# Second attention of a two-layer decoder block: the sum of a token's four gathered rows moved from VectorE into PSUM

## The chip, the cores and the metric

The kernel runs on one core of a Trainium2 chip. The metric is the time of one execution on the device in microseconds (us), the median of several runs; lower is better. TensorE (PE; its weight loads PEld) multiplies into PSUM, VectorE (DVE) and ScalarE (ACT) compute, GpSimd (POOL) computes and issues indirect DMAs (gathers), SyncE (SP) issues plain DMAs. Each engine runs its own program in order and waits on semaphores.

## The reference

For x of 128 sequences x 64 tokens x 128, in f32, and a context of the same shape:

```
x = x + attention0(layernorm(x), ctx, ctx)     # 16 heads of 8
x = x + ffn0(layernorm(x))                     # 32 experts, top 4, clipped swiglu, + own input
x = x + attention1(layernorm(x), ctx, ctx)     # 16 heads of 8, with rotary positions
x = x + ffn1(layernorm(x))                     # 8 experts, top 2
```

The first expert layer leaves its results as rows of a table in memory, one row per (token, expert) slot. A token's result is the sum of its four rows; that sum is added to x when the second attention starts.

## The kernel before

The 8192 tokens are 64 tiles of 128; X, the residual, stays in SBUF. The program is six stages, one after the other: attention 0, a sort of the slots, experts 0, attention 1, another sort, experts 1. The change lies in attention 1 alone (`attention(layer=1)`, about 868 to 1345 us of the profile).

An attention works on a pair of tiles at a time, 32 pairs, in a software pipeline that is written out by hand: each engine has a `body(i, on)` that is emitted for one value of i after the other, and in body i works on several pairs at once. `i.at(k)` is pair i+k, and `on(k)` says that this pair exists. Bodies run from -4 (on GpSimd from -5) to the end. The stages of pair n, with the body in which they run:

- Body n-5, GpSimd: the rows of pair n are gathered from the table `slot_results` into `gb`, of which there are two (even and odd pairs). There are eight indirect DMAs (L413) of 128 rows x 512 bytes, four ranks x two tiles. The order on GpSimd in body i (`body_with_gathers`) is: gather rank 0 of pair i+5, `scale_outputs` of pair i-2 (L455), gather rank 1, `scale_inputs` of pair i+3 (L426, L431), gather rank 2, `keep_top` of pair i-4, gather rank 3. Before rank 0 it waits until the buffer's former pair has been added to X.
- Body n-4, VectorE: `combine` waits for all eight gathers, sums the four rows (L549, a reduce over the rank) into `rows_sum` and adds them to X (L553).
- Body n-3, VectorE: `stats` of X (L528 to L541); GpSimd: `scale_inputs`, the power -0.5 of the variance, which waits for `stats`.
- Body n-2: ScalarE normalises, TensorE transposes X and the context (`inputs`, L912 and L914) into the bank `M_`.
- Body n-1: projections into `P_` and, with rotated weights, into `M_` (L919 and L920 in both cases); VectorE `rotate` (L618 twice in pairs, L629); ScalarE spreads keys and queries over the heads (L707).
- Body n: `scores` (L837), on VectorE four maxima (`score_unit`, L570), on TensorE their transposes (`maxima`, L848), transposed scores (`turned`, L862 and L874), ScalarE's exponentials.
- Body n+1: `values` (L893, L899), VectorE `divide` (L610, L612), TensorE `output`, VectorE `add_output` (L634) and `output_stats`.
- Body n+3: the rows for the next expert layer are transposed (`rows_turned`, L950, into the first half of `M_`), copied by ScalarE (L785, semaphore `tt`), and TensorE multiplies the gate (L962); then VectorE reads the logits (L585) and chooses the top 8.

The order on TensorE in body i (`body_with_rotation`) is: scores(i), values(i-1), projections(i+1) into `P_`, rows_turned(i-3), maxima(i), turned(i), projections(i+1) into `M_`, gate(i-3), next_values(i+1), output(i-1), inputs(i+2). The order on VectorE (`body_with_sums`) is: four score_unit(i), divide(i-1), the first half of the rotary product of pair i+1, rotate(i+1), read_logits(i-3), stats(i+3), combine(i+4), add_output(i-1), choose(i-3), output_stats(i-1).

`M_` is thus used by rows_turned, by the rotation and by inputs in turn, and its second half (columns 256 to 511) is free between inputs and the rotation.

Of the kernel before, what the change touches and what calls it, by code (L numbers as in the profile page):

```python
# [22 lines left out]
ALU = mybir.AluOpType  # L23
ACT = mybir.ActivationFunctionType
AX = mybir.AxisListType

P = 128
B, S, D = 128, 64, 128
# [10 lines left out]
E0, K0, F0 = 32, 4, 128  # L39
# [52 lines left out]
def hold(eng, sem, value):  # L92

    eng.wait_ge(sem, value)
    eng.nop(nofuse=True)  # L95


def build(nc, a, out, ts, ys, bias_parts):

    with ExitStack() as ctx:  # L100
# [9 lines left out]
        X = sb("X", [P, TILES, D])  # L110
# [12 lines left out]
        def part_of(name):  # L123
# [4 lines left out]
        ident, cos, sin, gate_w, max_to, den_of, bias_t, head_of, gate_b = (  # L128
            part_of(n) for n in ("ident", "cos", "sin", "gate_w", "max_to", "den_of", "bias_t", "head_of", "gate_b"))
# [19 lines left out]
        def carve(width, dt=F32):  # L149
            lo = place[0]  # L150
            place[0] += width if dt in (F32, I32, U32) else (width + 1) // 2
            assert place[0] <= ARENA, place[0]
            v = arena[:, lo:place[0]]
            return v if dt == F32 else v.bitcast(dt)
# [143 lines left out]
        gathered = [sem(f"gathered{q}") for q in range(2)]  # L298
# [6 lines left out]
        s = {n: sem(n) for n in names}  # L305

        def attention(layer):
# [19 lines left out]
                                               ("rs1", 2))}  # L327

            gb = carve2(2 * K0 * D) if layer else None
            rows_sum = carve(2 * D) if layer else None  # L330

            wq, wk, wv, wo = (Wm[:, 4 * layer + n, :] for n in range(4))
            bq, bk = bias_t[:, 2 * layer:2 * layer + 1], bias_t[:, 2 * layer + 1:2 * layer + 2]
# [2 lines left out]
            U_, O_, R_, M_, P_ = bank[0:4], bank[4], bank[5], bank[6], bank[7]  # L336
            base = layer * ITERS

            def tiles(buf, i):
                return buf[:, bass.ds(i.n * 2, 2), :]  # L340
# [20 lines left out]
            with nc.Block() as block:  # L361
# [43 lines left out]
                def _(pool):  # L405
                    def gather(i, k):

                        if k == 0 and i.n >= 2:

                            hold(pool, s["combined"], i.n - 1)  # L410
                        for j in range(2):
                            at, to = i.n * 2 + j, (j * K0 + k) * D
                            nc.gpsimd.indirect_dma_start(  # L413
                                out=gb[i.par][:, to:to + D], out_offset=None, in_=ys,
                                in_offset=bass.IndirectOffsetOnAxis(ap=slot[:, at, k:k + 1], axis=0),
                            ).then_inc(gathered[i.par], 16)
# [107 lines left out]
                def _(dve):  # L524
# [19 lines left out]

                    def combine(i):

                        q = i.par
                        hold(dve, gathered[q], (i.half + 1) * 16 * 2 * K0)
                        nc.vector.tensor_reduce(rows_sum.rearrange("p (i d) -> p i d", i=2),  # L549
                                                gb[q].rearrange("p (i k d) -> p i d k", i=2, k=K0), AX.X, ALU.add  # L550
                                                ).then_inc(s["row_sum"], 1)
                        hold(dve, s["row_sum"], i.n + 1)
                        nc.vector.tensor_tensor(tiles(X, i), tiles(X, i), rows_sum.rearrange("p (i d) -> p i d", i=2),  # L553
                                                ALU.add).then_inc(s["combined"], 1)

                    def offsets(i):

# [8 lines left out]
                    def score_unit(i, r):  # L566

                        g4 = i.g * UNITS
                        dve.wait_ge(s["score_psum"], g4 + r + 1)
                        nc.vector.tensor_reduce(mx[:].rearrange("p (w c) -> p w c", w=2)[:, :, 32 * r:32 * r + 4],  # L570
                                                U_[r][:, :].rearrange("p (w j k) -> p w j k", w=2, j=4), AX.X, ALU.max
                                                ).then_inc(s["score_max"], 1)
# [90 lines left out]
                    def body_with_sums(i, on):  # L663
                        nx, pv, p3 = i.at(1), i.at(-1), i.at(-3)
                        if on(0):
                            for r in range(UNITS):
                                score_unit(i, r)
                        if on(-1):
                            divide(pv)
                        if on(1):  # L670
                            dve.wait_ge(s["qk_psum"], nx.g + 1)
                            if not (isinstance(nx.n, int) and nx.n < 1):

                                dve.wait_ge(s["rope"], nx.n)
                            weigh(nx, QKe, P_, bq, bk, cos, "qk")
                            rotate(nx)
                        if on(-3):
                            read_logits(p3)
                        if on(3):
                            hold(dve, s["combined"], i.at(3).n + 1)  # L680
                            stats(i.at(3), small["st_a"], small["mv_a"], "stats_a", "moments_a")
                        if on(4):
                            combine(i.at(4))
                        if on(-1):
                            add_output(pv)
                        if on(-3):
                            choose(p3)
                        if on(-1):
                            output_stats(pv)
# [118 lines left out]
                def _(pe):  # L808
# [97 lines left out]
                    def inputs(i):  # L906

                        q = i.par
                        pe.wait_ge(ctx_in[q], (i.half + i.base // 2 + 1) * 16)
                        pe.wait_ge(s["normed"], i.g + 1)  # L910
                        for w in range(2):
                            nc.tensor.transpose(M_[:, w * P:(w + 1) * P], ctx_t[q][:, w * P:(w + 1) * P], ident[:])  # L912
                        for w in range(2):
                            last = nc.tensor.transpose(M_[:, (2 + w) * P:(3 + w) * P],  # L914
                                                       xn[q][:, w * P:(w + 1) * P], ident[:])
                        last.then_inc(s["cx_psum"], 1)

                    def projections(i, out_, wq, wk, done):
                        nc.tensor.matmul(out_[:, 0:2 * D], wq, CX[i.par][:, 2 * D:4 * D], start=True, stop=True)  # L919
                        nc.tensor.matmul(out_[:, 2 * D:4 * D], wk, CX[i.par][:, 0:2 * D], start=True, stop=True  # L920
                                         ).then_inc(done, 1)
# [24 lines left out]
                    def rows_turned(i):  # L946

                        pe.wait_ge(s["t_ready"], i.g + 1)
                        for w in range(2):
                            last = nc.tensor.transpose(M_[:, w * P:(w + 1) * P],  # L950
                                                       t[i.par][:, w * P:(w + 1) * P], ident[:])
                        last.then_inc(s["tt_psum"], 1)
# [13 lines left out]
                    def body(i, on):  # L966
# [31 lines left out]
                        if on(1):  # L998
                            next_values(nx)

                    def body_with_rotation(i, on):
                        ex, nx, pv, p3 = (i.at(k) for k in (2, 1, -1, -3))
                        if on(0):
                            scores(i)
                        if on(-1):
                            values(pv)
                        if on(1):
                            pe.wait_ge(s["cx"], nx.g + 1)
                            if on(0):

                                pe.wait_ge(s["vbd"], i.g + 1)
                            projections(nx, P_, wq, wk, s["qk_psum"])
                        if on(-3):
                            rows_turned(p3)
                        if on(-2):

                            pe.wait_ge(s["added"], pv.g)
                        if on(0):
                            maxima(i)
                            turned(i)  # L1020
                        if on(1):
                            if on(-3):

                                pe.wait_ge(s["tt"], p3.g + 1)
                            projections(nx, M_, Wm[:, 8, :], Wm[:, 9, :], s["rot_psum"])
                        if on(-3):
                            gate(p3)
                        if on(1):
                            next_values(nx)
                        if on(-1):  # L1030
                            if on(-3):

                                pe.wait_ge(s["logits"], p3.g + 1)
                            output(pv)
                        if on(2):
                            if on(1):

                                pe.wait_ge(s["rot"], nx.n + 1)
                            inputs(ex)

                    if not layer:
# [843 lines left out]
```

## Time and profile before

| | |
|---|---|
| Time, median of 3 runs | 1830.72 us (1826.79 to 1831.70) |
| Profiled execution: time / span | 1834.56 us / 1831.9 us |
| Mean granted TensorE clock | 0.92 |
| Busy over the whole span | PE 81%, PEld 60%, DVE 63%, ACT 49%, POOL 60% |
| Gathers of attention 1 (L413) | 256, 254.3 us of GpSimd |
| Row sums (L549) | 32, median 1940 ns |

Busy time is a sum over stages that have different limits, so the table says what each engine has to do and not which of them is waited for. The span counts from the first to the last instruction of the profiled execution. The granted clock is 1.00 at 2.4 GHz and 0.50 at 1.2 GHz. A row of busy time gives a stretch and its length, then the busy time of PE, PEld, DVE, ACT and POOL (with instructions), the granted clock, the DMA share and GB/s. A timeline row gives start, duration, engine, line, what is written from what, how many instructions were merged into it, and in brackets the idle time of that engine before it with what ended it.

### The profile page before, as it was taken

What the parts mean: (1) busy time and instruction counts of PE and PEld (TensorE: products, weight loads), DVE (VectorE), ACT (ScalarE), POOL (GpSimd) and SP (SyncE); (2) the same over time, 40 slices, a digit from 0 to 9 for tenths busy, and PEclk for the clock granted to TensorE, in tenths of its full rate; (3) what the DMA queues carried; (4) which work ended last, traced back from release to release, by engine and by line L of the source; (5) the groups of instructions that cost most, each with busy time, mean ns of one, the idle gap of its engine ahead of it and who ended that gap; (6) DMA issues with size and microseconds to landing.
All of it is one profiled execution on the core that took longest, in us unless ns stands there. A gap on an engine that the chain in (4) does not pass through costs nothing. (4 is left out here: it accounts for less than half of the span.)

```text
span 1831.9 us, 58162 instructions
## 1 busy us (share of the span) xinstructions
PE 1479.6 (81%) x21070; PEld 1104.2 (60%) x21071; DVE 1158.7 (63%) x3147; ACT 889.3 (49%) x2010; POOL 1102.3 (60%) x1438
## 2 busy tenths in 40 slices
PE   5999999739699999997277777777864799999960
PEld 4677777514477777775155555555642677777740
DVE  5777777679566666664378888888869222224432
ACT  2666666546233333332156666666545344444420
POOL 4677777400577777772777777677310776445766
PEclk9999999869899999998599999999985899999985
DMA  4211111000144444446242222112100233233332
GB/s 168 72 42 40 37 43 35 20 8 1 47 102 111 106 107 107 106 100 73 55 155 56 56 60 56 53 54 59 29 16 1 65 86 81 59 59 85 105 94 75
DMA packets 146836, 122.98 MB, mean 67 GB/s; under 512 B 27403, under 2 KB 132011, under 8 KB 145963
## 3 DMA queue, kind: packets, MB, share of 16 engines
q0 software_dynamic: 26112, 55.30, 13.8%
q1 hardware_dynamic: 120382, 65.58, 11.9%
q8 instruction: 68, 1.11, 0.3%
q10 hardware_dynamic: 240, 0.70, 0.1%
q14 instruction: 34, 0.28, 0.1%
HBM read 80.28 MB, written 41.23 MB: 66 GB/s over the span
## 5 line engine op out<-in xcount | busy, mean ns | idle before, releaser
L1427 POOL DMA_INDIRECT arena<-expert_rows,token_of_slot x432 | 415.7, 962 | 325.4 <-issue 219.8
L413 POOL DMA_INDIRECT arena<-slot_results,slot x256 | 254.3, 994 | 115.0 <-issue 86.5
L1800 DVE TENSOR_TENSOR arena<-bank,arena 128x352 f32<-128x352 f32 x144 | 74.7, 523 | 214.1 <-ACT arena L1779 213.9
L1733 PE MATMUL bank<-W,arena 128*128 x576 | 196.4, 464 | 0.9 <-ACT arena L1791 0.9
L1525 PE MATMUL bank<-W,arena 128*128 x576 | 175.4, 400 | 0.0
L699 ACT ACTIVATE arena<-bank 128x512 f32<-128x512 f32 x256 | 132.2, 603 | 87.4 <-PE bank L874 87.4
L570 DVE TENSOR_REDUCE mx<-bank 128x8 f32<-128x512 f32 x256 | 158.2, 679 | 13.7 <-PE bank L837 10.1
L1383 POOL DMA_INDIRECT arena<-slot_results,slot x128 | 121.5, 949 | 59.3 <-issue 43.3
L436 POOL TENSOR_TENSOR arena<-arena,fixed 128x1024 f32<-128x1024 f32 x64 | 121.4, 1917 | 55.8 <-ACT arena L717 55.8
L1747 PEld LDWEIGHTS bank<-W,arena 128*128 128x128 f32 (+1 forms) x864 | 114.2, 190 | 37.7 <-issue 30.2
L1747 PE MATMUL bank<-W,arena 128*128 (+1 forms) x864 | 120.5, 275 | 1.8 <-ACT arena L1786 1.8
L1733 PEld LDWEIGHTS bank<-W,arena 128*128 128x128 f32 x576 | 99.2, 192 | 32.8 <-issue 2.8
L707 ACT ACTIVATE arena<-arena,fixed 128x256 f32<-128x256 f32 x256 | 105.7, 495 | 26.3 <-DVE arena L629 26.3
L1353 PE MATMUL bank<-arena 128*128 128x288 f16 (+1 forms) x384 | 86.1, 394 | 39.1 <-ACT arena L1338 21.4
L1610 DVE TENSOR_SCALAR arena<-bank 128x256 f32<-128x256 f32 x144 | 61.1, 424 | 86.1 <-PE bank L1525 85.2
L1560 PE MATMUL bank<-W,arena 128*128 x576 | 114.2, 319 | 0.0
L610 DVE RECIPROCAL arena<-bank 128x256 f32<-128x256 f32 x64 | 111.7, 1746 | 2.4 <-PE bank L899 2.4
L1779 ACT ACTIVATE arena<-bank 128x352 f32<-128x352 f32 x144 | 66.7, 463 | 92.7 <-PE bank L1733 92.7
L1525 PEld LDWEIGHTS bank<-W,arena 128*128 128x128 f32 x576 | 89.6, 196 | 21.9 <-issue 1.7
L1785 ACT ACTIVATE arena<-bank 128x256 f32<-128x256 f32 x144 | 55.2, 383 | 84.6 <-PE bank L1758 84.6
L1560 PEld LDWEIGHTS bank<-W,arena 128*128 128x128 f32 x576 | 86.7, 190 | 10.4
L837 PE MATMUL bank<-arena 32*64 32x256 f32 x2048 | 72.6, 388 | 24.6 <-ACT arena L707 24.2
(197 smaller groups left out, 3468.7 us busy)
## 6 DMA issues: line engine op xcount, KB each, us to landing
slot_results<-arena SPq DMA_DIRECT2D x108, 256.0 KB
arena<-in_ctx SPq DMA_DIRECT2D x64, 128.0 KB
expert_rows<-arena SPq DMA_DIRECT2D x64, 128.0 KB, 1.9
arena<-expert_rows,token_of_slot POOLq DMA_INDIRECT x432, 2.6
arena<-slot_results,slot POOLq DMA_INDIRECT x384, 2.5
X<-in_x SPq DMA_DIRECT2D x32, 128.0 KB, 2.2
W<-in_w SPq DMA_DIRECT2D x4, 1024.0 KB
out_x<-arena SPq DMA_DIRECT2D x32, 128.0 KB, 1.8
```

The lines of the kernel that those rows point to most:

```text
L413: nc.gpsimd.indirect_dma_start(out=gb[i.par][:, to:to + D], out_offset=None, in_=ys, in_offset=bass.IndirectOffsetOnAxis(ap=slot[:, at, k: ...
L436: nc.gpsimd.tensor_tensor(dst[i.par].rearrange("p (b j k) -> p b j k", b=4, j=4), src[i.par].rearrange("p (b k) -> p b k", b=4).unsqueeze( ...
L570: nc.vector.tensor_reduce(mx[:].rearrange("p (w c) -> p w c", w=2)[:, :, 32 * r:32 * r + 4], U_[r][:, :].rearrange("p (w j k) -> p w j k", ...
L610: nc.vector.reciprocal(rec, O_[:, 2 * D:4 * D]).then_inc(s["o_recip"], 1)
L699: nc.scalar.activation(Pt[r], U_[r][:, :], ACT.Exp, scale=SCALE).then_inc(s["probs"], 1)
L707: last = nc.scalar.activation(dst[i.par].rearrange("p (b j k) -> p b j k", b=4, j=4)[:, :, j, :], src[i.par].rearrange("p (b k) -> p b k", ...
L1383: nc.gpsimd.indirect_dma_start(out=gb[q][:, at:at + D], out_offset=None, in_=ys, in_offset=bass.IndirectOffsetOnAxis(ap=slot[:, 2 * n + j, ...
L1427: nc.gpsimd.indirect_dma_start(out=XE[n % R][:, c * ROW:(c + 1) * ROW], out_offset=None, in_=ts, in_offset=bass.IndirectOffsetOnAxis(ap=to ...
L1525: last = nc.tensor.matmul(h, XT[i.par][:, c * P:(c + 1) * P], W0a[:, bass.ds(x_e, 1), :], start=False, stop=True, skip_group_check=True)
L1560: last = nc.tensor.matmul(y, AT[pv.par][:, c * P:(c + 1) * P], W0b[:, bass.ds(x_e, 1), :], start=False, stop=True, skip_group_check=True)
L1733: last = nc.tensor.matmul(H_[2 * r + u][:, 0:F1], XT[i.par][:, c * P:(c + 1) * P], W1a[:, bass.ds(x_e, 1), u * F1:(u + 1) * F1], start=Tru ...
L1747: last = nc.tensor.matmul(Y_[j.par][:, d * P:(d + 1) * P], AT[d % 2][0:f, k * P:(k + 1) * P], W1b[0:f, bass.ds(x_e, 1), k * P:(k + 1) * P] ...
```

## The change

The four rows are summed by four matmuls with the identity, which accumulate in the second half of `M_`. They stand in TensorE's body between rows_turned and maxima (`sum_rows`), so TensorE, and no longer VectorE, waits for the gathers of pair i+4. The add of the sum to X now reads PSUM, and `combine` stands on VectorE behind the four score_unit, ahead of divide. Two waits on `combined` are new on TensorE: before the projections into `M_`, and before `inputs` where there is no such projection. `sum_rows` waits for `tt` (or, in the first bodies, for the add of the pair before). GpSimd waits for `row_sum` where it waited for `combined`.

```diff
-            rows_sum = carve(2 * D) if layer else None
...
-                            hold(pool, s["combined"], i.n - 1)
+                            hold(pool, s["row_sum"], i.n - 1)
...
                     def combine(i):
 
-                        q = i.par
-                        hold(dve, gathered[q], (i.half + 1) * 16 * 2 * K0)
-                        nc.vector.tensor_reduce(rows_sum.rearrange("p (i d) -> p i d", i=2),
-                                                gb[q].rearrange("p (i k d) -> p i d k", i=2, k=K0), AX.X, ALU.add
-                                                ).then_inc(s["row_sum"], 1)
                         hold(dve, s["row_sum"], i.n + 1)
-                        nc.vector.tensor_tensor(tiles(X, i), tiles(X, i), rows_sum.rearrange("p (i d) -> p i d", i=2),
-                                                ALU.add).then_inc(s["combined"], 1)
+                        nc.vector.tensor_tensor(tiles(X, i), M_[:, 2 * D:4 * D].rearrange("p (i d) -> p i d", i=2),
+                                                tiles(X, i), ALU.add).then_inc(s["combined"], 1)
...
                             for r in range(UNITS):
                                 score_unit(i, r)
+                        if on(4):
+                            combine(i.at(4))
                         if on(-1):
                             divide(pv)
...
-                        if on(4):
-                            combine(i.at(4))
                         if on(-1):
                             add_output(pv)
...
+                    def sum_rows(i):
+
+                        hold(pe, gathered[i.par], (i.half + 1) * 16 * 2 * K0)
+                        rows = gb[i.par].rearrange("p (i k d) -> p i k d", i=2, k=K0)
+                        for k in range(K0):
+                            last = nc.tensor.matmul(M_[:, 2 * D:4 * D].rearrange("p (i d) -> p i d", i=2), ident,
+                                                    rows[:, :, k, :], start=(k == 0), stop=(k == K0 - 1),
+                                                    skip_group_check=True)
+                        last.then_inc(s["row_sum"], 1)
...
                             rows_turned(p3)
+                        if on(4):
+                            if on(-3):
+
+                                pe.wait_ge(s["tt"], p3.g + 1)
+                            elif far.n > 0:
+
+                                pe.wait_ge(s["combined"], far.n)
+                            sum_rows(far)
...
+                            if on(4):
+
+                                pe.wait_ge(s["combined"], far.n + 1)
                             projections(nx, M_, Wm[:, 8, :], Wm[:, 9, :], s["rot_psum"])
...
                                 pe.wait_ge(s["rot"], nx.n + 1)
+                            elif on(4):
+
+                                pe.wait_ge(s["combined"], far.n + 1)
                             inputs(ex)
```

## Rows read from the trace of the kernel before

**Rows 1.** Busy time by stretch: the pipeline filling, and the steady part of attention 1.

```profile
868.00:923.00 55.00, 17.88 (x169) 11.71 (x170) 17.62 (x37) 10.72 (x24) 41.99 (x47) 0.50 0.22 58
940.00:1313.00 373.00, 288.63 (x6586) 217.06 (x6586) 314.25 (x864) 235.06 (x556) 262.67 (x360) 0.97 0.23 67
```

**Rows 2.** Waits from 940 to 1240 us: total, times, longest.

```profile
PE bank L848 <- DVE mx L570: 42.8, 21, 2.2
```

**Rows 3.** Timeline of one round, 1084 to 1103 us.

```profile
1084.40 0.44 PE L848 MATMUL bank<-fixed,mx 128*128 128x128 f32 x2 [2.18 <-DVE mx L570]
...
1086.90 0.70 PE L919 MATMUL bank<-arena,Wm 128*128 128x256 f32 x2
...
1087.44 0.59 PE L920 MATMUL bank<-arena,Wm 128*128 128x256 f32 x2
...
1087.87 0.51 PE L962 MATMUL bank<-fixed,arena 128*128 128x8 f32 x4
...
1088.08 0.88 DVE L618 SCALAR_TENSOR_TENSOR arena<-bank,fixed 128x256 f32<-128x256 f32 x2 [0.82 <-PE bank L920]
...
1090.85 1.97 DVE L549 TENSOR_REDUCE arena<-arena 128x256 f32<-128x1024 f32 x1
...
1090.94 0.72 POOL L426 TENSOR_TENSOR arena<-arena,power 128x2 f32<-128x2 f32 x1 [0.44 <-DVE arena L541]
...
1091.56 1.12 PE L837 MATMUL bank<-arena 32*64 32x256 f32 x32 [0.58 <-ACT arena L707]
...
1093.03 0.43 DVE L553 TENSOR_TENSOR X<-X,arena 128x256 f32 x1 [0.21 <-DVE arena L549]
...
1093.37 0.42 DVE L634 TENSOR_TENSOR X<-bank,X 128x256 f32 x1
...
1095.43 2.47 DVE L570 TENSOR_REDUCE mx<-bank 128x8 f32<-128x512 f32 x4
...
1095.48 0.38 PE L950 MATMUL bank<-fixed,arena 128*128 128x128 f32 x2
...
1095.89 0.38 ACT L785 ACTIVATE arena<-bank 128x256 f32<-128x256 f32 x1 [0.84 <-PE bank L950]
...
1096.53 0.94 POOL L413 DMA_INDIRECT arena<-slot_results,slot  x1 [0.30 <-issue]
...
1097.96 0.44 PE L848 MATMUL bank<-fixed,mx 128*128 128x128 f32 x2 [2.10 <-DVE mx L570]
...
1101.88 0.88 DVE L618 SCALAR_TENSOR_TENSOR arena<-bank,fixed 128x256 f32<-128x256 f32 x2 [1.07 <-PE bank L920]
```

**Rows 4.** TensorE's timeline: scores that open bodies 2, 29 and 30.

```profile
940.22 1.12 PE L837 MATMUL bank<-arena 32*64 32x256 f32 x32 [1.46 <-ACT arena L707]
...
1320.39 1.12 PE L837 MATMUL bank<-arena 32*64 32x256 f32 x32 [0.58 <-ACT arena L707]
...
1332.34 1.12 PE L837 MATMUL bank<-arena 32*64 32x256 f32 x32 [0.58 <-ACT arena L707]
```

**Rows 5.** Timeline of the filling, 909 to 925 us.

```profile
909.65 0.94 POOL L413 DMA_INDIRECT arena<-slot_results,slot  x1 [0.30 <-issue]
...
912.23 1.89 DVE L549 TENSOR_REDUCE arena<-arena 128x256 f32<-128x1024 f32 x1 [5.41 <-DMA arena<-slot_results,slot]
...
917.10 0.69 PE L848 MATMUL bank<-fixed,mx 128*128 128x128 f32 x2 [3.95 <-DVE mx L570]
...
923.56 0.88 DVE L618 SCALAR_TENSOR_TENSOR arena<-bank,fixed 128x256 f32<-128x256 f32 x2 [5.74 <-PE bank L920]
```

**Rows 6.** Busy time of two neighbouring rounds; the clock is third from the end.

```profile
1176.00:1191.10 15.10, 11.82 (x252) 8.87 (x252) 12.14 (x34) 9.11 (x23) 10.03 (x15) 0.89 0.20 52
1191.10:1204.70 13.60, 10.46 (x249) 7.89 (x250) 11.64 (x34) 8.66 (x22) 10.32 (x14) 1.00 0.21 58
```

**Rows 7.** Timeline around pair 6's landing, 944 to 953 us.

```profile
944.90 0.94 POOL L413 DMA_INDIRECT arena<-slot_results,slot  x1 [0.30 <-issue]
...
952.62 1.99 DVE L549 TENSOR_REDUCE arena<-arena 128x256 f32<-128x1024 f32 x1 [0.42 <-DMA arena<-slot_results,slot]
```

More of the change, by code:

```diff
@@ L999, in body @@
                             next_values(nx)
+                    def sum_rows(i):
[6 more added lines that the diff above has]
+                        last.then_inc(s["row_sum"], 1)
                     def body_with_rotation(i, on):
-                        ex, nx, pv, p3 = (i.at(k) for k in (2, 1, -1, -3))
+                        ex, nx, pv, p3, far = (i.at(k) for k in (2, 1, -1, -3, 4))
                         if on(0):
```

## The prediction

> **What bounds the kernel now.** I read four views, in this order. First the busy time by stretch [rows 1]: the second attention's steady part (940 to 1313 us) keeps VectorE busy 314 of 373 us, TensorE 289, GpSimd 263, at a mean granted clock of 0.97; the filling of its pipeline (868 to 923) has GpSimd busy 42 of 55 us and TensorE at half clock. No engine is full, so waits decide. Second the waits [rows 2]: TensorE's longest is for the score maxima, 42.8 us in 21 rounds, some 2.0 us each. Third the timeline of one round [rows 3], which shows the loop that this wait belongs to. Call M the start of the maxima's transposes (L848), R the start of the rotation's second pair on VectorE (L618, which waited for L920). M to R is TensorE's work, 1084.40 to 1088.08 = 3.68 us (3.92 a round later, 1097.96 to 1101.88). R to the next M is VectorE's, 9.88 us, nearly without a gap: rope, statistics, the row sum (L549, 1.97), its add, the output's add, top-8, statistics, four score maxima (L570), and then L848 sets off. The scores themselves (L837) had ended at 1092.68, 2.75 us before L570 started. Last the rounds' starts by L837 [rows 4]: (1320.39 - 940.22)/27 = 14.08 us on average; a round of the tail, which has no row sum, lasts 11.95.
>
> So on this view the row sum is on the path, and taking it off should pay. The question is what the new place of the sum asks for.
>
> **The change, part by part.**
> 1. VectorE loses L549 (1.97 us) and the 0.21 us before its add, and the add (0.43) leaves the stretch R to M [rows 3]: some 2.5 us off that stretch. It would pay if nothing else ended later there.
> 2. VectorE gains an add that reads PSUM, now ahead of `divide`. L634 has the same form and lasts 0.42, 0.34 to the next start. It waits for the row sum, which ends some 0.2 us after M, where L570 ended just before M. The later chain moves by about 0.6 us, and L618 stood idle 0.82 to 1.07 for TensorE [rows 3]: free while that lasts, up to 0.6 us a round if not.
> 3. TensorE gains four f32 matmuls of 256 columns, two records each. By L919, L920 and what follows, starts lie 0.54, then 0.43 apart [rows 3]: 0.54 + 3 x 0.43 = 1.83 us. Bounds: 1.72 and 2.16. Ahead of them it waits for `tt` (L785, to 1096.27), which costs 0.4 to 0.65 after L950's stream. That alone fits into the wait of 2.10 us before L848, nearly.
> 4. The waits on `combined` before the second rotation matmuls and before `inputs` cost nothing in the steady part: the add ends some 0.7 us after M, L919 starts 2.50 after it. The write to X[pair] beside them is as before.
> 5. GpSimd waits for `row_sum` in place of `combined` before it fills a buffer again: both came a round earlier, no cost.
> 6. What decides: `sum_rows` in body i needs all eight gathers of pair i+4, and it is now held on TensorE ahead of the maxima, before the middle of the body, where `combine` had them at its end. GpSimd issues the last four of these gathers in its body i-1, behind `scale_inputs` of pair i+2 (L426), and L426 waits for VectorE's statistics of that pair, which come after R of body i-1. In [rows 3]: R at 1088.08, L426 at 1090.94 released by L541, the last gather (L413) at 1096.53 to 1097.47. From the start of a last gather to the row sum that waited for it, 909.65 to 912.23 = 2.58 us, 1.64 after its end [rows 5]. So pair i+4 lands at R + 2.86 + 6.53 + 1.64 = R + 11.03. TensorE gets there once L785 has ended, 1096.27, that is R + 8.2: it waits 2.8 us more, and behind it in TensorE's order stand the maxima's transposes, `turned` and the rotation, for which R itself waits. It is a loop through four engines and a DMA, and GpSimd can't run ahead, since L426 needs this round's R. Before, the reduce sat some 5.8 us behind the landing (about 1104.9, one mean round after L549's 1090.85, against 1099.1), so this loop had slack.
>
> **The sum.** A round in the new loop: M to R 3.68, to L426 2.86, to the end of the last gather 6.53, landing 1.64, start of the matmuls 0.06, the sum 1.83: 16.60 us. With M to R at the mean of both rounds shown (3.80) 16.7. I add 0.4 for the clock (below): 17.1, against 14.08 before, +3.0.
> The clock: TensorE stood idle 2.1 us before the maxima, and rounds with a stretch at 0.5 exist already; the one shown has a mean clock of 0.89 and 15.1 us, where its neighbour at 1.00 has 13.6 [rows 6], so a low stretch costs about 1.3 us (1.1 to 1.5). The new idle time, from the end of L950 (1095.86) to the landing, is 3.3 us. More low stretches must follow; I take one in three rounds beyond what there was, 0.4 us, between 0 and 1.3. By the Trainium skill (TensorE: Matmul & The Clock Gate, HAM oscillation), TensorE falls back to half speed when the gap between two bursts grows long enough, and does so in every round of such a loop; by that rule the sum would take the 1.3 and not the 0.4. The rows of before agree that gaps bring low stretches, but not in every round.
> Filling: pairs 0 to 3 are taken as they land, at GpSimd's pace, both before and after. But in body -1 the rotation now waits for pair 3: landed 912.23 [rows 5], four sums at half clock 3.6, the add 0.5, two rotation matmuls about 2: R(-1) at 918.3. Pair 4 lands 11.0 later, 929.3; sums at half clock, M(0) at 933; before it was 917.10. M(0) to R(0) was 6.46 at half clock; 5.5 if the clock rises earlier. R(0) is at 938.5 against 923.56: +15 (11 to 17).
> Weights: while the second layer's expert weights are loaded (4.5 MB by their shapes), pair 6, whose last gather started at 944.90, was taken at 952.62, 7.7 us later in place of 2.58 [rows 7]. Before, this had slack; now one round takes it: +5 (0 to 6).
> Tail: bodies 28 on have no sum on either side; body 28's maxima lose their old wait: -2.
> Total: 27 x 3.0 = 81.5, +15 +5 -2 = +99.5 us. The profiled execution's span is 1831.9, its time 1834.6, and the three runs' median, 1830.7, is 3.8 below that. So 1931 in span, and 1930 us by the median.
>
> By the Trainium skill (DMA: Bandwidth & Descriptors, Anatomy of one DMA) a GpSimd-issued DMA costs about 2.0 us and its bytes over 436 GB/s; for 64 KB that is 2.15, and an estimate with that in place of the 1.64 behind the gather's end adds 0.5 a round, some 14 us in all. The row measures 2.58 from the start of the issue and 1.64 from its end, and I go by it.
>
> **Rivals.**
> - The clock falls in every round: 16.7 + 1.3 = 18.0 us a round. 27 x 3.9 = 106, +17 +5 -2 = +126: 1957 us. For it: the longer gap. Against: with a period that walks against whatever paces the clock, some rounds should escape, as 2.1 us of idle did before.
> - No more low stretches than before, cheap filling: 16.6 a round, 27 x 2.5 = 68, +11 +0 -2 = +77: 1908 us.
> - The gathers aren't late, for instance because GpSimd gets further ahead than I read: TensorE binds. Its own loop is 11.95 [rows 4] + 1.83 + 0.65 for `tt` = 14.4, +0.35 a round, 9 us and the filling's 15: 1855 us. Against: the order on GpSimd is written out, and L426 is released by L541 in the rows.
> - The other side, faster: the sum hides wholly in the wait for the maxima and VectorE's 2.5 us come off. The floor is then 11.95 + 1.83 = 13.8, -0.3 a round: with no loss in filling 1822 us. It needs the landing at or before L950's end, R + 7.8, so 3.2 us earlier than the rows have it; from there on each 1 us of lateness costs 27 us.
>
> **How the numbers follow.** Chances: forecast 0.69, clock in every round 0.15, cheap clock and filling 0.11, gathers in time 0.03, faster 0.02. The predicted time is the first's, 1930; its own range is 1915 to 1947. The range 1903 to 1960 takes in the second and third, with the bounds of M to R and of the matmuls (1.72 to 2.16, -3 to +9 us); it leaves out some 0.1. The smallest difference that counts is 0.3%, 5.5 us. Slower 0.97; faster 0.02; within 0.3% 0.01.
>
> **What the new profile would show.** Right: `sum_rows` is a TensorE group of some 256 records whose idle time before it is ended by the DMA of the gathers, 2.5 to 3.5 us in nearly each of 28 rounds; the wait of L848 on L570 is gone; the distance from a last gather's start to the first sum's start is about 2.6 us; L426 still starts some 2.9 us after L618's second pair; rounds of 16.5 to 18 us; more low stretches than in 0.97; VectorE idle most before the new add. Wrong: rounds near 14, the sum's wait ended by L785 or absent, gathers that end well before L950. If the rounds are 16.6 exactly, my clock term is at fault; if the filling costs other than 15, my chain of body -1 is.

## The result and the profile after

The changed kernel takes 1956.7 us (median of 4, 1952.5 to 1966.3) against 1830.4 before: ratio 1.068, interval 1.065 to 1.072. The profiled execution's time is 1957.4 us and its span 1955.6, 123.7 more than before.

From the page of the profile, the engines' busy time and shares of the span, and TensorE's granted clock in 40 slices:

```profile
PE 1566.7 (80%) x21326; PEld 1173.0 (60%) x21327; DVE 1099.8 (56%) x3115; ACT 889.7 (45%) x2010; POOL 1091.1 (56%) x1438
...
PEclk9999999788999999985888888889896599999985
```

Busy time by stretch (columns as in [rows 1]): the filling, the steady part, and two single rounds.

```profile
868.00:923.00 55.00, 23.22 (x96) 15.59 (x96) 6.79 (x28) 5.47 (x13) 33.72 (x40) 0.55 0.17 44
960.00:1420.00 460.00, 348.26 (x6425) 265.65 (x6424) 250.88 (x794) 221.89 (x525) 248.57 (x348) 0.88 0.18 51
1163.30:1182.50 19.20, 14.77 (x257) 11.22 (x257) 10.23 (x35) 9.09 (x22) 10.08 (x15) 0.82 0.15 41
1218.40:1234.80 16.40, 12.26 (x262) 9.58 (x263) 9.92 (x32) 8.80 (x22) 9.88 (x14) 1.00 0.17 48
```

VectorE does less, 251 of 460 us where it was 314 of 373 [rows 1], and waits. The granted clock of the steady part is 0.88, not 0.97. One of the two rounds has a clock of 0.82 and lasts 19.2 us, the other 1.00 and 16.4.

Waits from 960 to 1400 us (total, times, longest), where [rows 2] had TensorE wait for the maxima:

```profile
DVE X L547 <- PE bank L1000: 174.9, 24, 12.0
...
POOL arena L425 <- DVE arena L540: 128.1, 24, 9.3
...
PE bank L1000 <- DMA arena<-slot_results,slot: 72.7, 23, 3.3
```

The wait of the maxima's transposes on the score maxima has gone from the list. TensorE now waits for the gathers, 3.2 us in each of 23 rounds, VectorE for the sum, and GpSimd for VectorE's statistics, 5.3 us a round, which it did for 0.4 in [rows 3].

The timeline of one round, to be read beside [rows 3]. M is again the start of the maxima's transposes (now L842) and R the start of the rotation's second pair on VectorE (now L612).

```profile
1162.73 0.72 POOL L425 TENSOR_TENSOR arena<-arena,power 128x2 f32<-128x2 f32 x1 [5.38 <-DVE arena L540]
...
1163.35 1.12 PE L831 MATMUL bank<-arena 32*64 32x256 f32 x32 [0.57 <-ACT arena L701]
...
1164.71 2.48 DVE L564 TENSOR_REDUCE mx<-bank 128x8 f32<-128x512 f32 x4
...
1167.68 0.38 ACT L779 ACTIVATE arena<-bank 128x256 f32<-128x256 f32 x1 [0.84 <-PE bank L944]
...
1168.32 0.94 POOL L412 DMA_INDIRECT arena<-slot_results,slot  x1 [0.30 <-issue]
...
1170.90 3.75 PE L1000 MATMUL bank<-arena,fixed 128*128 128x256 f32 x8 [3.25 <-DMA arena<-slot_results,slot]
...
1174.44 0.63 PE L842 MATMUL bank<-fixed,mx 128*128 128x128 f32 x2
...
1174.87 0.42 DVE L547 TENSOR_TENSOR X<-bank,X 128x256 f32 x1 [7.68 <-PE bank L1000]
...
1178.87 0.88 DVE L612 SCALAR_TENSOR_TENSOR arena<-bank,fixed 128x256 f32<-128x256 f32 x2 [0.67 <-PE bank L914]
...
1181.73 0.72 POOL L425 TENSOR_TENSOR arena<-arena,power 128x2 f32<-128x2 f32 x1 [6.13 <-DVE arena L540]
```

It reads as a chain that closes on itself. GpSimd sets off (L425) at 1162.73, and 6.53 us later, at 1169.26, its last gather (L412) ends. The sum (L1000) starts at 1170.90, 1.64 after that, released by the DMA, though `tt` was there since 1168.06 (L779). From the sum's start to M are 3.54 us, at the clock's lower level (1.80 at the higher one, see below), and from M to R 4.43. L425 starts again 2.86 after R. The five stretches add up to 19.00 us, from one L425 (1162.73) to the next (1181.73). The four score maxima (L564), for which M waited before, were done at 1167.19, 7.2 us ahead of M.

The scores that open bodies 3 and 28 of the changed kernel:

```profile
978.99 1.12 PE L831 MATMUL bank<-arena 32*64 32x256 f32 x32 [1.15 <-ACT arena L701]
...
1433.18 1.12 PE L831 MATMUL bank<-arena 32*64 32x256 f32 x32 [0.57 <-ACT arena L701]
```

That is (1433.18 - 978.99)/25 = 18.17 us a round; before, by the same bodies, 14.16 (952.96 to 1306.97). The span's 123.7 us are 26.0 up to body 3, 25 x 4.0 = 100.2 from there to body 28, and -2.5 after it.

### The profile page after: what moved, and what is told of

The parts are those of the page before. It is cut to its first block and busy times, and to the rows that moved or that the text cites. A ratio compares the mean times of both kernels' runs of the same rounds, so it can differ in the third digit from the quotient of the medians.

```text
span 1955.6 us, 58655 instructions
## 1 busy us (share of the span) xinstructions
PE 1566.7 (80%) x21326; PEld 1173.0 (60%) x21327; DVE 1099.8 (56%) x3115; ACT 889.7 (45%) x2010; POOL 1091.1 (56%) x1438
## 3 DMA queue, kind: packets, MB, share of 16 engines
q0 software_dynamic: 26112, 55.30, 12.9%
## 5 line engine op out<-in xcount | busy, mean ns | idle before, releaser
L412 POOL DMA_INDIRECT arena<-slot_results,slot x256 | 246.6, 963 | 114.9 <-issue 87.5
L1000 PE MATMUL bank<-arena,fixed 128*128 128x256 f32 x256 | 107.4, 593 | 128.9 <-DMA arena<-slot_results,slot 110.7
L564 DVE TENSOR_REDUCE mx<-bank 128x8 f32<-128x512 f32 x256 | 158.5, 682 | 17.8 <-PE bank L831 17.7
L1000 PEld LDWEIGHTS bank<-arena,fixed 128*128 128x128 f32 x256 | 73.5, 300 | 152.5 <-issue 137.4
L547 DVE TENSOR_TENSOR X<-bank,X 128x256 f32 (+1 forms) x32 | 13.6, 425 | 254.6 <-PE bank L1000 254.6
L1401 POOL DMA_INDIRECT arena<-slot_results,slot x128 | 121.4, 948 | 59.6 <-issue 43.3
L425 POOL TENSOR_TENSOR arena<-arena,power 128x2 f32<-128x2 f32 x64 | 46.0, 718 | 177.6 <-DVE arena L540 175.0
L1751 PEld LDWEIGHTS bank<-W,arena 128*128 128x128 f32 x576 | 99.3, 192 | 32.9 <-issue 2.8
```

Of the source, the lines that this page charges most:

```text
L412: nc.gpsimd.indirect_dma_start(out=gb[i.par][:, to:to + D], out_offset=None, in_=ys, in_offset=bass.IndirectOffsetOnAxis(ap=slot[:, at, k: ...
L1000: last = nc.tensor.matmul(M_[:, 2 * D:4 * D].rearrange("p (i d) -> p i d", i=2), ident, rows[:, :, k, :], start=(k == 0), stop=(k == K0 - ...
L1401: nc.gpsimd.indirect_dma_start(out=gb[q][:, at:at + D], out_offset=None, in_=ys, in_offset=bass.IndirectOffsetOnAxis(ap=slot[:, 2 * n + j, ...
L1751: last = nc.tensor.matmul(H_[2 * r + u][:, 0:F1], XT[i.par][:, c * P:(c + 1) * P], W1a[:, bass.ds(x_e, 1), u * F1:(u + 1) * F1], start=Tru ...
```

## The experiments

Each was timed beside the kernel before on the same chip, whose median moved between 1834 and 1837 us, so ratios are given. In the table, "round" is the mean from body 3 to body 28 by TensorE's scores in the profiled execution, and "clock" is the granted clock of the steady part.

| kernel | time, us | ratio to before (interval) | round | body 3 starts | clock |
|---|---|---|---|---|---|
| before | 1830.4 | | 14.16 | 953.0 | 0.97 |
| changed | 1956.7 | 1.068 (1.065 to 1.072) | 18.17 | 979.0 | 0.88 |
| 1 gathers first | 1835.1 | 1.000 (0.998 to 1.002) | 14.02 | 961.2 | 1.00 |
| 2 gathers first, in before | 1825.9 | 0.995 (0.993 to 0.997) | 13.71 | 955.3 | 0.99 |
| 3 one rank | 1905.0 | 1.038 (1.035 to 1.042) | 16.26 | 973.6 | 0.91 |
| 4 wait filled | 1921.5 | 1.048 (1.045 to 1.051) | 16.54 | 982.0 | 0.99 |
| 5 place alone | 1912.9 | 1.044 (1.038 to 1.049) | 16.54 | 972.8 | 0.82 |
| 6 late sum | 1878.7 | 1.025 (1.019 to 1.030) | 14.97 | 980.1 | 0.99 |
| 7 pair adds | 1808.8 | 0.987 (0.982 to 0.993) | 13.23 | 950.3 | 0.99 |
| 8 pair adds, gathers first | 1809.4 | 0.987 (0.981 to 0.992) | 13.20 | 956.1 | 0.98 |
| 9 half in PSUM | 1812.1 | 0.988 (0.985 to 0.990) | 13.26 | 963.6 | 0.99 |
| 10 pair adds moved | 1824.5 | 0.994 (0.992 to 0.996) | 13.49 | 961.5 | 0.97 |

**1. Gathers first.** Theory: the late landing closes a loop over four engines. Rival: the sum's work and waits on TensorE.

```diff
                             gather(i.at(5), 1)
+                            gather(i.at(5), 2)
+                            gather(i.at(5), 3)
                         if on(3):
                             scale_inputs(i.at(3))
-                        if on(5):
-                            gather(i.at(5), 2)
                         if on(-4):
                             keep_top(i.at(-4))
-                        if on(5):
-                            gather(i.at(5), 3)
```

> The changed kernel with one edit on GpSimd: all four ranks of a pair's gathers are issued ahead of scale_inputs in the body, so that none of them stands behind L425's wait for VectorE's statistics. If the lateness of the gathers in the loop GpSimd - TensorE - VectorE is the cause (my theory), the wait before the sum matmuls, 3.0 to 3.3 us a round after the change, is gone, TensorE binds with 11.95 + 1.83 + 0.65 = 14.4 us a round, the low clock goes with the wait, and the time is 1845 to 1870 us. If it is what the sum adds to TensorE and its new waits on tt and combined that costs (rival), the rounds stay above 17 us and the time above 1930.

Its steady part and one round:

```profile
960.00:1300.00 340.00, 297.30 (x6268) 232.34 (x6272) 242.72 (x780) 216.91 (x513) 238.64 (x338) 1.00 0.21 58
```

```profile
1161.73 0.38 PE L942 MATMUL bank<-fixed,arena 128*128 128x128 f32 x2
...
1162.15 0.38 ACT L777 ACTIVATE arena<-bank 128x256 f32<-128x256 f32 x1 [0.96 <-PE bank L942]
...
1162.68 1.97 PE L998 MATMUL bank<-arena,fixed 128*128 128x256 f32 x8 [0.56 <-ACT arena L777]
...
1164.48 0.38 PE L840 MATMUL bank<-fixed,mx 128*128 128x128 f32 x2
...
1164.87 0.42 DVE L545 TENSOR_TENSOR X<-bank,X 128x256 f32 x1 [3.33 <-PE bank L998]
```

The sum (L998) now starts on the copy L777 with 0.56 us idle, never on a DMA, and M (L840) follows 1.80 later. The whole 6.8% is gone with the order of GpSimd's instructions; TensorE still does all four matmuls. The rival falls. The time is 10 us under the expectation's lower end, since TensorE's own loop is 14.0 and not 14.4 and the filling costs 8 us and not 15.

**2. The same reorder in the kernel before**, as a control.

> The kernel before with the same reorder on GpSimd, as a control of the reorder by itself. The reduce sat 5.8 us behind the landing, so on my theory nothing moves: 1825 to 1836 us. If the order on GpSimd is worth something of its own (rival: scale_inputs or scale_outputs come late behind eight gathers, or the filling gets longer), the time moves by more than 5 us.

The time lies in the range I gave, but the kernel before, timed beside it, took 1837.0: the reorder isn't neutral, it is worth 0.5%. The round is 13.6 us most of the time, where 13.65 and 14.0 alternated, and of the 25 rounds two have a stretch at the lower clock (15.3 and 14.9 us) where the kernel before has seven (14.9 to 15.3 us); these five rounds are over half of the gain. Set against this control, experiment 1 is 0.5% slower: what the move costs when the gathers are early.

**3. One rank.** Leaves out ranks 1 to 3 of the sum; the gathers stay.

```diff
-                        for k in range(K0):
+                        for k in range(1):
...
-                                                    rows[:, :, k, :], start=(k == 0), stop=(k == K0 - 1),
+                                                    rows[:, :, k, :], start=True, stop=True,
```

> The changed kernel with one matmul per pair in place of four; it leaves out ranks 1 to 3 of the sum. All eight gathers are still issued and waited for. If the loop through the gathers sets the round, the three matmuls lie behind the landing and on the loop: 1.3 us a round less at full clock, up to 2.6 at half, so 35 to 70 us less than the changed kernel, 1887 to 1922 us. If the matmuls were hidden and only the wait cost, the time stays at 1957.

Some 52 us less than the changed kernel: the matmuls behind the landing are on the loop. The round is 1.9 us shorter for three matmuls fewer, between their price at full (1.3) and at half clock (2.6).

**4. The wait filled** with five matmuls whose result is overwritten.

```diff
+                            if on(-3) and on(1):
+                                for _ in range(5):
+                                    nc.tensor.matmul(M_[:, 2 * D:4 * D], ident, CX[nx.par][:, 0:2 * D],
+                                                     start=True, stop=True, skip_group_check=True)
                             sum_rows(far)
```

> The changed kernel with five further matmuls of 256 columns on TensorE, between the wait on tt and the wait for the gathers, into the half of the bank that the sum then overwrites: 2.2 us of work inside a wait of 3.2. If the idle time is what brings TensorE's clock down, and this makes rounds of 18.3 out of 16.5, the added work makes the kernel faster: rounds of 16.5 to 17.3, 1905 to 1935 us, clock of the steady part above 0.94. If the low clock isn't what lengthens the round, the time stays within 5 us of 1957 or grows.

```profile
960.00:1385.00 425.00, 370.27 (x6784) 285.41 (x6769) 252.43 (x802) 225.67 (x533) 252.24 (x353) 0.99 0.20 58
```

```profile
1151.86 2.43 PE L1028 MATMUL bank<-arena,fixed 128*128 128x256 f32 x10 [0.47 <-ACT arena L779]
...
1154.74 1.97 PE L1000 MATMUL bank<-arena,fixed 128*128 128x256 f32 x8 [0.46 <-DMA arena<-slot_results,slot]
...
1156.55 0.38 PE L842 MATMUL bank<-fixed,mx 128*128 128x128 f32 x2
```

TensorE is given 2.4 us more to do each round (L1028). It waits 0.46 for the gathers in place of 3.25, the sum takes 1.81 to M (L842) in place of 3.54, and the kernel is some 35 us faster than the changed one. The round is 16.54 at a clock of 0.99, and TensorE still waits for the gathers: this is the loop without the clock. The other 1.63 us a round of the changed kernel are the clock's, which falls with the idle wait and stays up when the wait is filled.

A wait of this length doesn't bring the clock down every time. In the changed kernel 22 of the 25 rounds have a granted clock of 0.82 to 0.91, and three have 1.00, one of them this, behind a wait of 3.10:

```profile
1217.64 0.72 POOL L425 TENSOR_TENSOR arena<-arena,power 128x2 f32<-128x2 f32 x1 [5.03 <-DVE arena L540]
...
1225.85 1.97 PE L1000 MATMUL bank<-arena,fixed 128*128 128x256 f32 x8 [3.10 <-DMA arena<-slot_results,slot]
...
1227.65 0.38 PE L842 MATMUL bank<-fixed,mx 128*128 128x128 f32 x2
...
1234.14 0.72 POOL L425 TENSOR_TENSOR arena<-arena,power 128x2 f32<-128x2 f32 x1 [3.61 <-DVE arena L540]
```

From L425 to L425 it lasts 16.50 us, where the round at 0.82 lasted 19.00.

**5. The place alone.** VectorE keeps its reduce, now into two buffers in turn; `combine` moves behind the score maxima.

```diff
                                 score_unit(i, r)
+                        if on(4):
+                            combine(i.at(4))
...
-                        if on(4):
-                            combine(i.at(4))
                         if on(-1):
                             add_output(pv)
```

> The kernel before, the sum still VectorE's reduce, with combine moved to the changed kernel's place, behind the four score maxima and ahead of divide (two buffers for the row sum). TensorE gets no work. By the loop theory the place alone closes the loop: the gathers land at R + 11.0, the reduce, the add, divide and the first rotary product follow, 5.6 us, so a round lasts about 16.7 us plus what the clock loses, and the time is 1900 to 1960 us. If it is TensorE's work or its waits that make the change slow (rival), the rounds stay near 14 and the time within 15 us of 1830.

```profile
1160.73 0.94 POOL L413 DMA_INDIRECT arena<-slot_results,slot  x1 [0.30 <-issue]
...
1161.23 0.38 PE L848 MATMUL bank<-fixed,mx 128*128 128x128 f32 x2
...
1163.35 1.95 DVE L549 TENSOR_REDUCE arena<-arena 128x256 f32<-128x1024 f32 x1 [2.59 <-DMA arena<-slot_results,slot]
...
1165.53 0.42 DVE L553 TENSOR_TENSOR X<-X,arena 128x256 f32 x1 [0.23 <-DVE arena L549]
...
1168.00 1.65 DVE L618 SCALAR_TENSOR_TENSOR arena<-bank,fixed 128x256 f32<-128x256 f32 x4
...
1171.63 0.72 POOL L426 TENSOR_TENSOR arena<-arena,power 128x2 f32<-128x2 f32 x1 [3.54 <-DVE arena L541]
```

The last gather starts at 1160.73, the reduce (L549) at 1163.35, 2.62 later, released by the DMA; M (L848) isn't held and goes at 1161.23, but R, inside L618's pairs, comes behind reduce, add and divide. No work was added to TensorE, and the kernel is 4.4% slower: the ring comes from the place in the body, not from the engine. TensorE's work isn't on this ring (L618's four records run without a wait), so here its low clock, 0.82, costs nothing that shows. The round is 16.54 us where I expected 16.7 and more, the same as in experiment 4. The other 2.4% of the change's 6.8 are about what the clock costs there, 1.63 us a round.

**6. Late sum.** `sum_rows` behind turned, `combine` behind the first rotary product, GpSimd as in the changed kernel.

```diff
-                            sum_rows(far)
...
                             turned(i)
...
+                            sum_rows(far)
```

> The changed kernel with sum_rows behind turned, ahead of the rotation's projections, and combine on VectorE behind the first rotary product; the order of the gathers is as in the changed kernel. By the loop theory TensorE then comes to the sum at about R + 10.5, the gathers land at R + 11.0, and the rotation follows 3.5 us later: rounds of 14.5 to 14.9, 1840 to 1870 us, with an idle time before the sum of under 1 us. If the sum's work were the cause and not when it asks for the gathers, the time stays above 1930.

```profile
1134.75 0.38 PE L843 MATMUL bank<-fixed,mx 128*128 128x128 f32 x2
...
1135.58 0.94 POOL L412 DMA_INDIRECT arena<-slot_results,slot  x1 [0.30 <-issue]
...
1138.22 1.97 PE L1001 MATMUL bank<-arena,fixed 128*128 128x256 f32 x8 [0.58 <-issue]
...
1140.41 0.42 DVE L547 TENSOR_TENSOR X<-bank,X 128x256 f32 x1 [3.04 <-PE bank L1001]
...
1142.06 0.88 DVE L612 SCALAR_TENSOR_TENSOR arena<-bank,fixed 128x256 f32<-128x256 f32 x2 [1.22 <-PE bank L915]
```

The last gather starts at 1135.58 and the sum (L1001) at 1138.22, 2.64 later, after 0.58 us of idle. The view doesn't put this idle time to the DMA, but the distance is that of a landing (2.58 in [rows 5]), so the sum just meets it. M (L843) is free of it. The round, 14.97, is 0.1 over what I expected; the time misses by 9 us, because the filling is as long as the changed kernel's (body 3 at 980.1), which I had not put in. The sum stands some 2.9 us of TensorE's work later in the same body (from M to the end of `turned`), and that takes away 3.2 of the 4.0 us a round.

**7 and 8. Pair adds**, in the kernel before: the reduce as two plain adds. Experiment 8 has the gathers first as well.

```diff
-                        nc.vector.tensor_reduce(rows_sum.rearrange("p (i d) -> p i d", i=2),
-                                                gb[q].rearrange("p (i k d) -> p i d k", i=2, k=K0), AX.X, ALU.add
...
+                        rows = gb[q].rearrange("p (i k d) -> p i (k d)", i=2, k=K0)
+                        nc.vector.tensor_tensor(half_sum.rearrange("p (i d) -> p i d", i=2), rows[:, :, 0:2 * D],
+                                                rows[:, :, 2 * D:4 * D], ALU.add).then_inc(s["row_sum"], 1)
...
+                        nc.vector.tensor_tensor(rows_sum.rearrange("p (i d) -> p i d", i=2), halves[:, :, 0:D],
+                                                halves[:, :, D:2 * D], ALU.add).then_inc(s["row_sum"], 1)
```

> The kernel before with the reduce on VectorE (1.94 us, which reads the four ranks at a stride) split in two plain adds of 512 and 256 elements per row: 0.69 by the rope's add and 0.42, so about 0.8 us less per round where VectorE is on the path from R to M. If that path sets the round in the kernel before, as my reading had it, rounds of 13.2 to 13.4 and 1800 to 1815 us. If something else sets it (rival: the clock or GpSimd, whose round needs about 12.9), the time stays above 1820.

> The same with the gathers ahead of scale_inputs on GpSimd. The reorder alone was worth 0.5% in the kernel before, so 1792 to 1810 us if the two add up; if GpSimd's own work (8 x 1.25 us of gathers and 2.9 of powers and copies, 12.9 us) now binds, no better than the pair adds alone.

```profile
1108.74 0.69 DVE L551 TENSOR_TENSOR arena<-arena 128x512 f32<-128x512 f32 x1
1109.54 0.42 DVE L555 TENSOR_TENSOR arena<-arena 128x256 f32<-128x256 f32 x1
1110.17 0.43 DVE L558 TENSOR_TENSOR X<-X,arena 128x256 f32 x1 [0.20 <-DVE arena L555]
```

In experiment 7 the sum lasts 1.22 us (1108.74 to 1109.96) in place of 1.97, 0.75 less, and the round falls by 0.93. That is more than was taken off, because two rounds have a stretch at the lower clock where the kernel before has seven; the rounds at full clock fall from 13.8 to 13.1 on average, 0.7. So VectorE's stretch from R to M did bound the kernel before, and the change went for the right work. In experiment 8 the reorder adds nothing on top. Most of its rounds last 12.9 to 13.0 us, which is GpSimd's own pace (busy 247 of 340 us, and 0.3 us behind each issue), and two of 15.2 and 17.0 with a low clock take back what that gains.

**9. Half in PSUM.** Experiment 1, with the first half of the sum on VectorE and two matmuls.

```diff
-                        hold(pe, gathered[i.par], (i.half + 1) * 16 * 2 * K0)
-                        rows = gb[i.par].rearrange("p (i k d) -> p i k d", i=2, k=K0)
-                        for k in range(K0):
+                        hold(pe, s["half"], i.n + 1)
+                        rows = half_sum[i.par].rearrange("p (i k d) -> p i k d", i=2, k=2)
+                        for k in range(2):
```

> The changed kernel with the gathers ahead of scale_inputs, and the sum shared: VectorE, which then idles 3.3 us a round before its add, adds ranks 0 and 1 to ranks 2 and 3 (0.69 us, behind the score maxima), and TensorE sums the two halves with two matmuls in place of four. With the gathers first TensorE set the round at 14.0 us with clock 1.00; two matmuls less are 0.86 us, so rounds of 13.2 us and 1808 to 1820 us. If the sum's matmuls weren't on TensorE's loop there (rival), the time stays at 1835.

As expected, a round lasts 13.26 us: in experiment 1 TensorE bound. This is the change's idea made to pay, and it ends where the pair adds do.

**10. Pair adds moved** to the changed kernel's place, gathers first.

> The pair adds on VectorE with the gathers first, and with combine moved behind the score maxima (the place that cost 4.4% when the gathers were late). With the gathers early the place should be harmless or good: M to R is then VectorE's, 3.0 + 1.6 = 4.6 us, R to the next scores 3.5, scores to M 4.5, 12.6 together, under GpSimd's 12.9. So rounds of 12.9 to 13.1, 1795 to 1812 us. If the place costs by itself, the time is above 1825.

A wait from 960 to 1290 us:

```profile
DVE arena L549 <- DMA arena<-slot_results,slot: 30.5, 19, 2.8
```

It misses its expectation by 12 us. Rounds start at 12.0 us (bodies 3 to 7) and then mostly last 13.5 to 14. VectorE again waits for the gathers, 1.6 us in each of 19 rounds. With the gathers first the place is no longer ruinous (4.4% slower without them), but it still asks for them sooner than GpSimd delivers. Why the rounds go past GpSimd's 12.9 I have not found.

## Why the prediction came out as it did

It was right in direction and mechanism, and 1956.7 lies in the range (1903 to 1960), at its upper end; the forecast of 1930 is 27 us low (24 in the span). The rounds make up the whole of it: in the profiled executions the 27 rounds from body 1 to body 28, without the weights' load, lost 108.7 us against the kernel before, where the sum had 81.5, while the filling, the load and the tail together came out 3 us cheaper.

- VectorE's 2.5 us off the stretch R to M: that stretch did bound the kernel before (experiment 7 takes 0.75 us off it, and the rounds at full clock are 0.7 shorter), and taking it off is worth nothing here, as argued.
- The loop through GpSimd (step 6), R + 11.03 for the landing: right to 0.05 us. In the round shown, R to L425 2.86, to the last gather's end 6.53, landing 1.64. Undoing the order (1), moving the demand for the gathers (5, 6) and shortening what lies behind the landing (3) each move the time as the loop says.
- The loop's length without the clock, 16.6 to 16.7 us: measured 16.54 (experiment 4).
- The step that failed is the size of the clock term, "I take one in three rounds beyond what there was, 0.4 us". It measured 1.63 us a round (18.17 against 16.54), 1.2 more, some 33 us over 27 rounds; the shorter loop gives back some 4 of them. Both of its factors were too low: 22 of the 25 rounds had a stretch at 1.2 GHz, and such a round cost not 1.3 but some 1.9 us on average (1.63 x 25/22), and 2.5 in the one shown (19.00 against 16.50), with all the work behind the gap on the loop. I read the wait before as evidence for mild effects, while the wait went from 2.1 to 3.3 us.
- The rival "the clock falls in every round", to which I gave 0.15, had this mechanism right, all but three rounds. That it names 1957, the measured time, is in part luck: it has 18.0 us a round where 18.17 were measured, and a filling 4 us dearer than it was.
- The Trainium skill (TensorE: Matmul & The Clock Gate, HAM oscillation) has TensorE fall back to half speed in every round of a loop whose gap between two bursts is long enough. The trace agrees in 22 of 25 rounds, and experiment 4, in which the gap is filled, has a clock of 0.99.
- The filling: the rows that answer to [rows 5], and the scores that open body 1, last of the changed kernel and then of the kernel before:

```profile
911.80 3.75 PE L1000 MATMUL bank<-arena,fixed 128*128 128x256 f32 x8 [6.24 <-issue]
...
918.25 0.88 DVE L612 SCALAR_TENSOR_TENSOR arena<-bank,fixed 128x256 f32<-128x256 f32 x2 [1.38 <-PE bank L914]
...
929.04 3.75 PE L1000 MATMUL bank<-arena,fixed 128*128 128x256 f32 x8 [2.53 <-issue]
...
932.58 0.63 PE L842 MATMUL bank<-fixed,mx 128*128 128x128 f32 x2
...
936.87 0.88 DVE L612 SCALAR_TENSOR_TENSOR arena<-bank,fixed 128x256 f32<-128x256 f32 x2 [2.77 <-PE bank L914]
...
940.36 1.33 PE L831 MATMUL bank<-arena 32*64 32x256 f32 x32 [1.90 <-ACT arena L701]
```

```profile
927.04 1.12 PE L837 MATMUL bank<-arena 32*64 32x256 f32 x32 [1.90 <-ACT arena L707]
```

R(-1) was forecast at 918.3 and came at 918.25; pair 4's landing at 929.3, came at 929.04; M(0) at 933, came at 932.58; R(0) at 938.5, came at 936.87, since M(0) to R(0) took 4.29 and not 5.5. Body 1 starts 13.3 us late against the 15.
- The weights' load: body 2's round is 22.4 us, 4.2 over the mean, against the 5. Pair 6's last gather starts at 961.66 and its sum at 968.56, 6.9 us later in place of 2.6, while the DMA share is 0.85 (last number but one of the second view). The weights' two transfers were issued at 955.8 and 956.3. That it is they that hold the gathers is inferred from the times; no run leaves them out.

```profile
961.66 0.94 POOL L412 DMA_INDIRECT arena<-slot_results,slot  x1 [0.30 <-issue]
...
968.56 3.60 PE L1000 MATMUL bank<-arena,fixed 128*128 128x256 f32 x8 [7.72 <-issue]
```

```profile
955.00:965.00 10.00, 4.60 (x120) 2.94 (x118) 4.35 (x16) 5.06 (x13) 6.57 (x8) 1.00 0.85 324
```

- The landing: 1.64 us from the end of the issue in the round shown, 2.58 from its start, as in [rows 5]. By the Trainium skill (DMA: Bandwidth & Descriptors, Anatomy of one DMA) the estimate was 2.15; counted from the end of the issue it would have been 0.5 too much.
- The four matmuls, 1.83 us to M: 1.80 to 1.81 at full clock (experiments 1 and 4), 3.54 at half.
- "TensorE binds, 14.4" if the gathers are in time: 14.02 (experiment 1). The floor was 0.4 too high, most of it in the 11.95: that was a round of the kernel before's tail, and the same round of experiment 1 lasts 11.6. With 1.80 for the sum and 0.56 for `tt` that makes 13.96.

What stays open: why the reorder on GpSimd gains 0.5% in the kernel before, the fewer rounds with a low clock among it; why three rounds of the changed kernel keep the full clock; and experiment 10's rounds.

## What to carry to other kernels

Before work is moved to an idle engine, ask not only what it costs there but when, in the order of that engine, it asks for its inputs: a step placed ahead of others holds all of them, and if its input is issued behind a wait on their results, the pipeline becomes a ring. Trace that ring once, from the moved instruction back to itself, with durations from rows; here the sum was right to 0.2 us, and moving the gathers ahead of one wait on another engine undid the whole loss. And count an idle gap on TensorE twice: as time, and as the lower clock of the work behind it. Here gaps of 3.2 us came with a clock of 0.88 and 1.6 us a round, gaps of 2.1 us with 0.97, and gaps of some 0.5 us with 0.99 to 1.00.

## What the runs showed that I had not expected

- Adding 2.4 us of useless matmuls a round to TensorE made the changed kernel some 35 us faster (1921.5 against 1956.7), with a granted clock of 0.99 in place of 0.88.
- The row sum as a strided reduce of 128x1024 to 128x256 takes 1.94 us on VectorE; as adds of 512 and 256 elements it takes 1.22, wait between them included, and the kernel gains 1.3%.
- A reorder that changes no dependence on the path I had read, gathers ahead of the powers on GpSimd, gave 0.5%.
